# Peak turning and piece order in the paired-head cross attention of a decoder kernel

## What is computed

```python
def _L3_xattn_ref(x, z, Wq, Wkv, Wo):
    Q = (x @ Wq.T).reshape(B, xN, NUM_HEADS, HEAD_DIM)          # 16 heads of 16
    KV = (z @ Wkv.T).reshape(B, zN, 2, NUM_HEADS, HEAD_DIM)     # z: the 375 rows of context
    attn = jnp.einsum('bqhd,bkhd->bhqk', Q, KV[:, :, 0]) * SCALE
    attn = jax.nn.softmax(attn, axis=-1)
    O = jnp.einsum('bhqk,bkhd->bqhd', attn, KV[:, :, 1]).reshape(B, xN, DIM)
    return O @ Wo.T
```

## Time and profile before

| | us |
|---|---|
| median of three runs | 2354.99 |
| the profiled execution's own time | 2357.41 |
| its span | 2355.4 |
| PE busy in the span | 2037.8 (87%) |
| DVE busy | 1332.3 (57%) |
| ACT busy | 840.4 (36%) |
| POOL busy | 715.1 (30%) |
| stage of layer 1, from its first product to its last sum into x | 737.19 to 944.33 |
| the same of layer 3 | 2034.32 to 2241.33 |

### The profile page before, as it was taken

The page is one execution under the profiler, slowest core; times in us unless marked ns, Lnnn a source line. Parts: engine busy times, 40 slices in busy tenths (PEclk is TensorE's granted clock), DMA queues, the critical chain, the costliest instruction groups (busy, mean ns, idle before and its releaser), DMA issues.

```text
span 2355.4 us, 59884 instructions
## 1 busy us (share of the span) xinstructions
PE 2037.8 (87%) x24096; PEld 1488.1 (63%) x24096; DVE 1332.3 (57%) x3559; ACT 840.4 (36%) x3000; POOL 715.1 (30%) x1608
## 2 busy tenths in 40 slices
PE   8999998989987877898978798998999998787744
PEld 4899998867565655467866655665645555465523
DVE  6667676755265675545645615784370403567587
ACT  2455554533173333212334514664111112133322
POOL 3566664221011444101345503330000002345511
PEclk9555556999997999799998988998999999699956
DMA  3000001003000000300020000000200000000000
GB/s 134 4 5 5 5 5 77 2 21 158 4 2 8 8 12 2 134 1 23 1 110 22 2 1 8 11 8 2 113 35 1 0 0 4 7 8 12 2 0 16
DMA packets 8033, 57.35 MB, mean 24 GB/s; under 512 B 792, under 2 KB 5248, under 8 KB 5984
## 3 DMA queue, kind: packets, MB, share of 16 engines
q1 hardware_dynamic: 7760, 53.54, 5.9%
HBM read 52.62 MB, written 0.92 MB: 23 GB/s over the span
## 4 chain that ended last, share of the span: by engine, by line
PE 68%; DVE 17%; issue 6%; ACT 5%; POOL 3%; DMA 1%; POOLq 0%; DVEq 0%; SPq 0%; ACTq 0%
PE banks L274 42%; PE banks L1395 9%; PE banks L279 5%; PE banks L2028 3%; DVE memory L2128 3%; PE banks L1548 1%; PE banks L2035 1%; DVE memory L2146 1%; DVE memory L1278 1%; DVE memory L3054 1%; DVE memory L1497 1%; ACT memory L2118 1%; ACT memory L2109 1%; PE banks L968 1%; PE banks L1699 1%
## 5 line engine op out<-in xcount | busy, mean ns | idle before, releaser
L274 PE MATMUL banks<-memory 128*112 128x256 f32 (+9 forms) x4192 | 1147.0, 427 | 143.6 <-ACT memory L2109 39.3
L274 PEld LDWEIGHTS banks<-memory 128*128 128x128 f32 (+4 forms) x4192 | 698.7, 194 | 502.2 <-issue 340.7
L1395 PE MATMUL banks<-memory 128*128 128x8 bf16 (+2 forms) x10752 | 313.2, 175 | 7.8 <-DVE memory L1480 1.4
L279 PE MATMUL banks<-memory 112*112 112x112 f32 (+3 forms) x1328 | 219.3, 283 | 112.1 <-DVE memory L855 27.7
L1395 PEld LDWEIGHTS banks<-memory 128*128 128x128 bf16 x10752 | 300.1, 104 | 21.5 <-POOL memory L1454 11.7
L279 PEld LDWEIGHTS banks<-memory 112*112 112x112 f32 (+3 forms) x1328 | 156.9, 157 | 205.6 <-issue 64.9
L2118 ACT ACTIVATE memory<-banks 125x672 f32<-125x672 f32 x128 | 93.5, 731 | 238.2 <-PE banks L2035 238.2
L1497 DVE TENSOR_REDUCE memory<-banks 128x48 f32<-128x192 f32 x448 | 122.0, 291 | 61.9 <-PE banks L1395 41.3
L2128 DVE TENSOR_REDUCE memory<-banks 112x2 f32<-112x750 f32 x128 | 120.4, 941 | 44.4 <-PE banks L2028 42.5
L2196 POOL TENSOR_TENSOR memory<-memory 125x224 f32<-125x224 f32 x128 | 84.1, 657 | 180.6 <-ACT memory L2118 179.5
L2028 PE MATMUL banks<-memory 32*112 32x375 f32 x512 | 123.0, 554 | 3.4 <-DVE memory L2143 1.6
(11 more groups left out here) (266 smaller groups left out, 2909.7 us busy)
## 6 DMA issues: line engine op xcount, KB each, us to landing
memory<-in_l2x SPq DMA_DIRECT2D x1, 7680.0 KB, 21.2
memory<-in_l2f SPq DMA_DIRECT2D x1, 7168.0 KB, 20.2
memory<-in_l1f SPq DMA_DIRECT2D x1, 4617.0 KB, 14.8
memory<-in_ctxT SPq DMA_DIRECT2D x24, 187.5 KB
memory<-in_l2f SPq DMA_DIRECT2D x1, 4096.0 KB, 12.8
memory<-in_l3f SPq DMA_DIRECT2D x1, 3073.0 KB, 22.1
memory<-in_l2a SPq DMA_DIRECT2D x1, 3072.0 KB, 19.5
memory<-in_l0f SPq DMA_DIRECT2D x1, 2304.0 KB, 9.1
```

The source lines that it names most:

```text
L274: ins = self.nc.tensor.matmul(out, weights[i], acts[i], start=i == 0, stop=i == n - 1)
L279: return self.nc.tensor.transpose(out, in_, self.ident[0:n, 0:n])
L1395: ins = self.nc.tensor.matmul(own[:, part:3, at:at + B], self.whh[:, part, l, j, g * P:(g + 1) * P], self.upper[l][:, 0:3 - part, j * B:(j ...
```

## The change

Four things change in the order of `Cross`, and nothing in what is computed.

- In a step, `peak` of pair n + 1 is yielded behind `cross` of pair n instead of ahead of it.
- The maxima of pair n + 2 become a step of their own, `top`, between the two; DVE thus takes them ahead of the add of pair n + 1. In `CrossL3` the `row` step of DVE comes ahead of `top`.
- `plan`: y moves from step 3 to step 4, vv from step 6 to step 5, kk(1) from step 7 to step 6; v stays in step 7.
- In the prologue `stats` comes ahead of `parity`.

```diff
-    prologue = (("parity", 0), ("stats", 0), ("xn", 0), ("kk", 0), ("xT", 0), ("q", 0))
+    prologue = (("stats", 0), ("parity", 0), ("xn", 0), ("kk", 0), ("xT", 0), ("q", 0))
     second = (("kk", 1, 0), ("stats", 0, 1), ("vv", 0, 0), ("v", 2, 0), ("xn", 0, 1))
-    plan = ((("xT", 0, 1), ("stats", 0, 2)), (), (("q", 0, 1),), (("kk", 0, 1), ("xn", 0, 2), ("y", 0, -1)), (), (),
-            (("vv", 0, 1),), (("kk", 1, 1), ("v", 2, 1)))
+    plan = ((("xT", 0, 1), ("stats", 0, 2)), (), (("q", 0, 1),), (("kk", 0, 1), ("xn", 0, 2)), (("y", 0, -1),),
+            (("vv", 0, 1),), (("kk", 1, 1),), (("v", 2, 1),))
...
             b, i = divmod(n, 8)
+            yield "cross", b, n
+            yield "top", b, n + 2
             if n + 1 < self.pairs:
                 yield "peak", (n + 1) // 8, n + 1
-            yield "cross", b, n
             if n >= 4 and n % 4 < 2:
...
         if step == "score":
             self.dve_peaks(i)
-        elif step == "cross":
-            if i + 2 < self.pairs:
-                self.dve_peaks(i + 2)
+        elif step == "top":
+            if i < self.pairs:
+                self.dve_peaks(i)
```

More of the change, by code:

```diff
@@ L2149, in dve_more @@
                             ALU.mult).then_inc(*s.oT_ready.up())
[L2150 to L2153, removed]
         else:
```

## The result

The changed kernel takes 2340.96 us (median of four runs, 2340.21 to 2342.93) against 2354.33 beside it: a ratio of 0.9942, 95% interval 0.9925 to 0.9959. The gain is 13 us. The time lies inside the range of 2319 to 2343, but 10 us above the 2331 forecast, 3 outside the likeliest case (2324 to 2338) and next to the rival *half gain* (2342). The changed kernel's profiled execution took 2340.21.

A forecast was written before the change was run, and what follows sets the result against it. PE stalls behind ACT's reading of the keys and DVE's maxima were taken as the loss; 2.00 us a middle batch, 12.0 a stage, 24 in all took the profile from 2357.41 to 2333.4, the median to 2331, range 2319 to 2343.

The forecast's parts named there:

- half gain: Rival: lone transpose costs 0.24 in steps 0, 4, 5; covers of 6, 7 fail by 0.2; 2342 us, chance 0.14.
- The stall of bank 7: Steps 3 and 7: the second piece waits for ACT's reading of the keys; 28 waits, 39.3 us in all.
- it doesn't do what it says: Rival: waits for bank 7 are not the loss, steps 3 and 7 stay over 3.5; within 3 us, chance 0.05.
- the add becomes the bound and the kernel is slower: Rival: S waits for DVE's maxima, then add; at 0.35 more per DVE-bound step about 2363 us; chance 0.05.
- A middle batch: Eight steps of a batch between a stage's first and last: 20.84 against 22.84 us, 12.0 gained a stage.
- The lone transpose: One transpose standing alone between X and W on PE: 0.08 more in step 0, 0.24 within steps 4 and 5.
- the thin covers of steps 6 and 7: Margin between a bank being read and kk or v wanting it: 0.1 to 0.2 us.
- The ring's handover: DVE from maxima to add, between one S and the next: 0.86 or 0.97 by the add's half; ring 2.19 or 2.30.
- DVE's pieces ahead of the maxima in steps 1 and 2: xT copy and stats, then the norm: maxima start at 1.27 and 1.95, steps last 2.60 and 3.28.
- The last batch: Last batch of each stage: y, hidden in step 3 before, costs 0.8 us in step 4.
- the clock: Rival: a ring with long PE idle would run part-way at 1.2 GHz instead of 2.4; no separate chance given.
- The prologue: Start of each stage: xn blocked by POOL's clearing, or 3 us earlier; taken as 0, -2 and +6 for the range.

The follow-up runs named there:

- e1: The kernel before with the new `plan` alone; peak, maxima and prologue as before: 2328.92 us, ratio 0.9891.
- e2: The changed kernel with the old `plan` and old prologue, so only `peak` and `top` are moved: 2356.29 us, ratio 1.0005.
- e4: The changed kernel with DVE's add of pair n + 1 ahead of the maxima of pair n + 2: 2321.63 us, ratio 0.9860.
- e10: The changed kernel unaltered, run and profiled once more: 2340.48 us, ratio 0.9946.

## Why the prediction came out as it did

**The stall of bank 7: right.** Two stalls per middle batch were the loss, the plan removes them, and the 28 waits are 2. That 28 was two for each of seven batches was a lucky count: in each stage one stands in the prologue, six in step 3 and seven in step 7, so 26 could go. e1 shows that they are worth the whole gain, e2 that nothing else in the change is. Neither "it doesn't do what it says" nor "the add becomes the bound and the kernel is slower" happened.

**A middle batch: 20.84 forecast, 21.04 measured.** The steps read, measured less forecast: +0.06, -0.06, -0.11, +0.01, +0.04, +0.06, +0.06, +0.13. Three terms are mis-sized, and that the sum is only 0.2 off is partly luck, since they have different signs.
- *The lone transpose.* I charged 0.08 in step 0, and nothing for its place in steps 4 and 5. Measured between e1 and the changed kernel it is 0.13 to 0.16 in each of the three steps in which PE is full (0, 4, 5), because between X and W it costs PE more than ahead of X. The sums for steps 4 and 5 had its full 0.24 in them and so came within 0.06. *Half gain* had the direction of step 0's; its other leg, the thin covers of steps 6 and 7, did not fail (that of step 7 does in e4, by 0.28).
- *The ring's handover.* The terms were 0.97 to the maxima, 0.86 or 0.97, 0.28, 0.08. The rows give 0.93, then 0.86 or 0.97, then 0.40 to 0.42 from the add's start to S, so the signal behind the add is 0.14 and not 0.08; with the 0.04 too much in the first term it came out even, 2.19 in step 3, where two errors cancel. Step 7 missed by 0.13 since I gave the short handover to every lower-half add, and it has the long one (0.97).
- *DVE's pieces ahead of the maxima in steps 1 and 2.* I had the maxima start 1.27 and 1.95 into the steps; they start 1.16 and 1.79 into them (807.09 and 810.26). That is 0.11 and 0.16 too much, which covers the signal's 0.05 or so and leaves the steps 0.06 and 0.11 shorter than forecast.

Over twelve middle batches, of which the sixth of each stage gained only 1.54, that is 3 us of the forecast 24: 20.9 came.

**The last batch: -0.8 forecast, -2.0 and -1.8 measured.** This term is mis-sized by its clock. I had put y's cost in step 4 at its length at 1.00. Behind the idle that I named under the rival *the clock* (2.09 in before, 2.01 in after) and dismissed with the middle batches, W and y of step 4 run at 0.50: 0.56 and 0.70 longer than the 0.79 and 1.12 at 1.00. Nor had y hidden in step 3 before: at a mean clock of 0.53, PE was busy in all 3.61 of that step. Both stages together lost 2.2 more than forecast.

**The prologue: 0 forecast, +0.7 and +1.1 in the lead-ins.** I asked whether xn or the clearing would be first. About xn I was right: it starts 5.3 us into the stage of layer 1 (744.58), as before (5.2). The term that I had left out is ACT's reading of the keys. It waits for the last of the mask instructions, which now stand between stats and xn and run into the clearing (3.68 us, above), and xn's transposes wait until that reading has freed bank 7: they start 6.4 us in, where it had been 5.7. The lower bound that I kept, -2, just held it (-1.8).

**Those terms together** are 3 + 2.2 + 1.8 = 7.0 short; the first batches gave 0.5 more than their 0.75 each, and the tail of layer 3 was 0.9 shorter. That leaves 5.8, the difference between 24 and 18.2 (the parts are rounded).

**From the stages to the median.** The forecast took the median to lie 2.4 below the profiled execution in both kernels. Beside the new runs, before's profile lay 3.1 above its median (2357.41 to 2354.33), and after's 0.75 below (2340.21 to 2340.96): 17.2 between the profiles is 13.4 between the medians. e10's stages, 2.3 longer than those of the first profile (1.7 of it in the first batches), say the same: a single profile of this kernel stands for the others within about 3 us, and the sum should have been widened by that.

**What would show it.** The keys' waits, steps 3, 4, 5 and 7, and S waiting for the add all showed; that the add's start goes by its half did not hold in step 7.

**What I had not weighed** is that the order itself could be a loss. The forecast of 20.84 and 2331 was met, by e1 with 20.65 and 2328.9, a kernel without the turned order. I priced "the ring saves T but pays the handover" in steps 1 and 2 and let it stand as even, without asking what the same plan would give in the old order: there T costs PE 0.15 less in the full steps, and steps 3 and 7, bound by the ring, take 2.21, where the turned ring gives 2.20 and 2.32.

## What to carry to other kernels

When a change has two parts, price each alone, and the first one with the second left out: here one part was the whole gain, and the other ate some of it. Of two instructions on one engine, first should stand the one that opens the next round (the add, 0.28 long), not the one that is longer and a step ahead (the maxima, 0.94): turning just these two gave 19 us more. And work that is moved out of a stall into a full step costs its length at the clock that the stall leaves behind; at the last batch of these stages it was better left in the stall, by 0.8 to 1.1 us each.

## What the runs showed of the hardware

- An add on 128 partitions lasts as long as one on 64 (0.26 to 0.28), and a DVE instruction whose inputs start where the last read from the same memory started begins 0.11 sooner behind the maxima (0.86 for 0.97).
- From the end of a DVE add to the first product that waits for it it is 0.14 to 0.15 (803.17 + 0.27 to 803.59, 813.44 + 0.26 to 813.84), against 0.06 from the maxima to the transpose's weight load in the earlier trace rows.
- A DVE instruction of two elements a partition lasts 3.68 beside POOL's clearing of buffers, though the clearing only writes; with the clearing held back it lasts 0.17.
- In a step that PE fills, a single transpose costs TensorE 0.13 to 0.16 more between two sets of tiled products than it does at the step's end (behind a full-width product in two of the three steps).
- In two executions of one kernel the clock stood at 0.50 until 30.9 and 30.6 us behind a stage's first product, and until 33.1 and 34.1; the first batches differed by 0.8 and 0.9 us.
